# One weight cast moved behind the first norm, sixty unread products ahead of the first transposes, two means and one rounding moved, in a two-layer GNN kernel

## The chip, the cores and the metric

The kernel runs on one core of a Trainium2 chip. The metric is the device time of one execution in microseconds; the median over several executions is what versions are compared by. TensorE's clock has two levels, 1.2 and 2.4 GHz.

## The reference

The program has 1,250 nodes of 1,024 features, 20,000 edges sorted by destination, and two pre-norm layers with a residual each:

```python
h = relu(layernorm(x))
e = sigmoid(h @ wenc.T + benc)                 # 1250 x 500
agg = segment_sum((e @ conv)[src] * edge_weight, dst)
x = x + (agg + e @ lin.T) @ wdec.T + bdec
h = relu(layernorm(x))
y = h @ W.T + b                                # 1024 x 1024
x = x + gcn_normalized_sum_with_self_loops(y, src, dst)
```

Only the first line and the encoder product `h @ wenc.T` lie in the stretch that the change touches; the sparse adjacency is built beside them.

## The kernel before

All five engines run programs written out by hand; they meet only in semaphores (`wait_ge`, `then_inc`), and each engine executes strictly in the order of its own program. A `Signal` is a semaphore whose events must be raised in a listed order.

**Numbers in two parts.** Every fp32 operand of a product is split in a rounded high part (fp32r) and the remainder. For the activations these are `zhi` (ScalarE, `z_hi`) and `zlo` (VectorE, `z_lo`); for the four blocks of encoder weights `wehi` and `welo` (`wenc_lo`, VectorE). `wehi` 0 and 1 are cast by GpSimd, 2 and 3 by ScalarE (`wenc_hi`). A product of 1,024 long rows is three passes over eight slices: high by high, low by high, high by low.

**Blocks.** The nodes are ten blocks of 125 rows (`xn`, six buffers). For each block the first norm needs a mean and a variance: VectorE takes them for blocks 0, 1, 2 and 4 (`norm_stats`), ScalarE for the rest (`block_mean`, then `block_var`, into `wide`, about a microsecond each). `norm_step(n)` on VectorE turns the sums of two blocks into a scale and a shift by a chain of twelve tiny dependent instructions. `z_relu` (ScalarE) applies them in two halves; block 1 alone is done by VectorE (line 968, signal `relu_v`, without the ReLU, which `z_hi` makes up for). TensorE then transposes the block into PSUM (`turn_z`, eight transposes, line 1275), and `z_hi` and `z_lo` read it from there.

**Slots.** After the first two blocks the three big engines walk through a list of 30 slots: slots 0 to 19 are the encoder's (five groups of two blocks by four weight blocks), the last ten the conv product's. Slot s has on TensorE one encoder product (24 matmuls of 250 columns), the windows of adjacency batches listed in `adjs[s]`, and the transposes of a block (`turn_at`: blocks 2 and 3 in slot 3, block 4 in slot 6, block 5 in slot 7). The last pass of a product is held back until `zlo` is there. On ScalarE slot s has `enc_sigmoid(s)`, some means, variances and ReLUs, `z_hi` of the block transposed, and `adj_evac(u)`, which copies the finished window group u out of PSUM bank 3 + u % 3 (lines 642 and 643, tiles `C` and `A`). TensorE may start window group u only when group u - 3 is evacuated. On VectorE slot s has `hot_batch` (builds one-hot tiles `m_hot`, `s_hot` for the windows), `z_lo`, `norm_step`, `enc_lo(s)` (`hlo`, remainder of the sigmoid).

**Adjacency input.** Early TensorE products spread destination samples (`spread`), ScalarE counts them twice (`count_samples`, lines 593), VectorE makes row numbers (`find_windows`), GpSimd fetches edge rows by four indirect DMAs (`gather`: `sdw`, `ww`) and VectorE makes keys of them (`edge_keys`, `kf`).

The place where ScalarE starts, before the slots:

```python
        z_relu(0, 0)
        z_relu(0, 1)
        for k in range(2):
            for h in range(2):
                z_hi(k, h)
        block_mean(3)
        block_var(3)
        wenc_hi(2)
```

Of the kernel before, what the change touches and what calls it, by code (L numbers as in the profile page):

```python
# [20 lines left out]
FB = 4  # L21
# [18 lines left out]
SCRATCH = 4096  # L40
NXN = 6
NHOT = 3
BANKS = [(0, 0, 500), (1, 500, 1000), (2, 1000, 1250)]

SBUF0 = 4224
# [56 lines left out]
def build(nc, x, src, dst, ew, dst_s, sd_rows, w_rows, wenc, benc, conv, lin, wdec, W, b, out):  # L102
# [5 lines left out]
    def signal(name, events, by=1):  # L108
        return Signal(sem(name), events, by)
# [19 lines left out]
    identh = small("identh", [128, 128], F16, 2)  # L129
# [174 lines left out]
    def one(n):  # L304
        return [(i,) for i in range(n)]
# [36 lines left out]
    z_turned = signal("z_turned", BH)  # L342
    zhi_ok = signal("zhi_ok", BH)
    zlo_ok = signal("zlo_ok", BH)
    whi_p = signal("whi_p", one(2))
    whi_a = signal("whi_a", [(2,), (3,)])
    wlo_ok = signal("wlo_ok", one(FB))
    enc_done = signal("enc_done", GF)
    hhi_ok = signal("hhi_ok", GF)
# [167 lines left out]
    def gpsimd(p):  # L517
        p.memset(identf[:, :], 0.0).then_inc(*made_p.up("identf0"))
        p.wait_ge(*made_p.at("identf0"))
        p.affine_select(out=identf[:, :], in_=identf[:, :], compare_op=ALU.not_equal, fill=1.0, base=0,  # L520
                        pattern=[[-1, 128]], channel_multiplier=1).then_inc(*made_p.up("identf"))
        p.iota(thr[:, :], [[WD * HW, 2]], base=0, channel_multiplier=WD,
               allow_small_or_imprecise_dtypes=True).then_inc(*made_p.up("thr"))

        for g in range(NG - 1):
            p.memset(f32(hhi[g][:, 0, :]), 1.0).then_inc(*one_row.up(g))
        p.wait_ge(*d16_ok.at())
        p.iota(iota_s[:, :, :], [[1, 128], [0, GB]], base=0, channel_multiplier=0,
               allow_small_or_imprecise_dtypes=True).then_inc(*made_p.up("iota"))

        def gather(t):
            p.wait_ge(*row_ok.at(t))
            where = bass.IndirectOffsetOnAxis(ap=row_i[0:HW, t:t + 1], axis=0)
            p.indirect_dma_start(sdw[0:HW, t].rearrange("p a e -> p (a e)"), None, sd_rows, where
                                 ).then_inc(*d_gat[2 * t].up())
            p.indirect_dma_start(ww[0:HW, t, :], None, w_rows, where).then_inc(*d_gat[2 * t + 1].up())

        for f in range(2):
            p.wait_ge(*d_we[f].at())
            p.tensor_copy(wehi[f][:, :, :], we32[f][:, :, :]).then_inc(*whi_p.up(f))  # L540
        for t in range(2):
            gather(t)

        p.wait_ge(*flag_ok.at())
        general = p.value_load(flag[0:1, 0:1])
        with p.If(general > 0):
            p.wait_ge(*win_done.at(NWIN - 1))
            p.wait_ge(*conv_done.at(NB - 1))
            p.wait_ge(*edge_ok.at())
            p.iota(gi_d[0:PB, :], [[1, N]], base=0, channel_multiplier=0, allow_small_or_imprecise_dtypes=True  # L550
                   ).then_inc(*g_made.up(0))
            p.memset(gz[0:PB, :], 0.0).then_inc(*g_made.up(1))

        p.wait_ge(*win_done.at(NWIN - 1))
        p.wait_ge(*settled.at())
        p.memset(f32(ouhi[0][:, 0, :]), 1.0).then_inc(*one_row0.up())
        p.wait_ge(*A_put.at(NU - 1))
        p.wait_ge(*made_v.at("loops"))
        for k in range(NB):
            d_ap = C[0:PB, k, k * PB:(k + 1) * PB]  # L560
            p.tensor_tensor(d_ap, d_ap, loops[0:PB, 0:PB], ALU.add).then_inc(*diagC.up(k))

        def split_W(t):
            p.wait_ge(*Whi_ok.at(t))
            p.tensor_tensor(Wlo[t][:, :], W32[t][:, :], f32(Whi[t][:, :]), ALU.subtract).then_inc(*Wlo_ok.up(t))

        for k in range(NB - 1):
            for c in range(2):
                p.wait_ge(*t32_ok.at(k, c))
                cs = slice(512 * c, 512 * c + 512)  # L570
                p.tensor_tensor(glo[k][0:PB, cs], t32[(2 * k + c) % 4][0:PB, :], ghi[k][0:PB, cs], ALU.subtract
                                ).then_inc(*glo_p.up(k, c))
            if k == 1:
                split_W(0)
                split_W(1)
            if k == 3:
                split_W(2)
        for t in range(3, KB):
            split_W(t)
# [3 lines left out]
    def scalar(a):  # L583
# [33 lines left out]
        def z_hi(k, h):  # L617
            g, i = divmod(k, 2)
            a.wait_ge(*z_turned.at(k, h))
            if g >= 2:  # L620
                a.wait_ge(*enc_done.at(g - 2, FB - 1))
            a.activation(zhi[g % 2][:, 4 * h:4 * h + 4, i * PB:i * PB + PB],  # L622
                         ps[turn_bank(k, h)][:, 0:4 * PB].rearrange("p (k n) -> p k n", n=PB), ACT.Relu
                         ).then_inc(*zhi_ok.up(k, h))
# [29 lines left out]
        for k in range(2):  # L654
            for h in range(2):
                z_hi(k, h)
        block_mean(3)
        block_var(3)
        wenc_hi(2)
        for s, slot in enumerate(SLOTS):  # L660
            if s == 1:
                for k in range(2, 4):
                    for h in range(2):
                        z_relu(k, h)
                wenc_hi(3)
            if s == 2:
                for k in range(2, 4):
                    for h in range(2):
                        z_hi(k, h)
            if s in (2, 6, 7):  # L670
                k = {2: 5, 6: 5, 7: 8}[s]
                if s == 6:
                    z_relu(k, 0)
                    z_relu(k, 1)
                else:
                    block_mean(k)
                if s == 2:
                    block_var(k)
            done = [w // WD for i in adjs[s] for w in windows_of(i) if w % WD == WD - 1]
            for u in done[:(len(done) + 1) // 2]:  # L680
                adj_evac(u)
            if slot[0] == "enc":
                enc_sigmoid(s)
            for u in done[(len(done) + 1) // 2:]:
                adj_evac(u)
            if s == 5:
                a.wait_ge(*key_turn.at(0))
                a.activation(edge_k[:, :, :].rearrange("p k (t w) -> p (k t) w", t=2),
                             ps[3][:, :].bitcast(BF16)[:, 0:512].rearrange("p (k w) -> p k w", w=128)[:, :, 0:HW], ACT.Copy
                             ).then_inc(*edge_ok.up())  # L690
            if s in (5, 8, 9, 12, 13):
                k = {5: 4, 8: 6, 9: 7, 12: 8, 13: 9}[s]
                z_relu(k, 0)
                z_relu(k, 1)
            for k in range(4, NB):
                if turn_at[k] == s:
                    z_hi(k, 0)
                    z_hi(k, 1)
            if s in (3, 6, 9):
                block_mean({3: 6, 6: 7, 9: 9}[s])  # L700
            if s in (3, 6, 8, 10):
                block_var({3: 6, 6: 7, 8: 8, 10: 9}[s])
            if s in (17, 18):
                js = slice(2 * s - 34, 2 * s - 32)
                a.wait_ge(*d_cv.at())
                a.activation(cvhi[:, js, :], cv32[:, js, :], ACT.Copy).then_inc(*cvhi_ok.up(s - 17))
            if s == 19:
                a.wait_ge(*d_lin.at())
                a.activation(lnhi[:, :, :], ln32[:, :, :], ACT.Copy).then_inc(*lnhi_ok.up())
            if slot[0] == "conv":  # L710
                conv_evac_hi(slot[1])
# [101 lines left out]
    def vector(v):  # L813
# [64 lines left out]
                                       ).then_inc(*zlo_ok.up(k, h))  # L878

        def wenc_lo(f):  # L880
            v.wait_ge(*(whi_p if f < 2 else whi_a).at(f))
            v.tensor_tensor(welo[f][:, :, :], we32[f][:, :, :], f32(wehi[f][:, :, :]), ALU.subtract).then_inc(*wlo_ok.up(f))  # L882

        def enc_lo(s):
# [368 lines left out]
    def tensor(t):  # L1253
        def mm(o_ap, lhsT, rhs, start, stop):
            return t.matmul(o_ap, lhsT, rhs, start=start, stop=stop)  # L1255
# [34 lines left out]
        def enc(s, ws):  # L1290
            g, f = SLOTS[s][1:]
            i = g % 2
            o_ap = slot_bank(s)[0:PB, 0:GN]
            t.wait_ge(*(whi_p if f < 2 else whi_a).at(f))

            def one_pass(k, kind, start, stop):
                if kind == "lw" and g == 0 and k == 0:
# [21 lines left out]
        def first_hi(f):  # L1319

            o_ap = slot_bank(f)[0:PB, 0:GN]
            t.wait_ge(*(whi_p if f < 2 else whi_a).at(f))
            for k in range(KB):
                mm(o_ap, wehi[f][:, k, :], zhi[0][:, k, :], k == 0, False)
                mm(o_ap, wehi[f][:, k, :], zlo[0][:, k, :], False, False)
# [49 lines left out]
        for r in range(5):  # L1375
            ins = mm(ps[r][0:HW, 0:500], identh[0:5, r:r + 1].to_broadcast([5, HW]), d16[0:5, :], True, True)
        ins.then_inc(*spread.up())
        t.wait_ge(*made_p.at("identf"))
        turn_z(0)
        turn_z(1)  # L1380
# [314 lines left out]
```

## Time and profile before

| what | value |
|---|---|
| time, three runs | 501.79, 502.46, 503.77 us; median 502.46 us |
| the profiled execution | 501.87 us, of which span 500.1 us |
| busy TensorE matmul | 482.2 us, 96% of the span |
| busy VectorE, ScalarE, GpSimd | 252.3, 190.5, 56.1 us |
| the first matmul of the program, the first transpose | 3.32 us, 12.90 us |
| first encoder product; first adjacency window behind slot 8's encoder product | 16.41 us; 50.96 us |

In the profile a line number is that of the instruction's source; `PE` is TensorE's matmuls, `PEld` its weight loads, `DVE` VectorE, `ACT` ScalarE, `POOL` GpSimd. The figure in square brackets behind an instruction is how long its engine sat idle ahead of it and what ended that. The span starts with the first instruction, and the time outside it is 1.8 us here.

### The profile page before, as it was taken

The numbers are of one execution on the slowest core, as the hardware profiler recorded it, in microseconds if no ns is written. First come the engines' busy times: TensorE is split into PE (matmuls) and PEld (weight loads), VectorE is DVE, ScalarE is ACT, GpSimd is POOL, SyncE is SP. The second block draws the span as 40 slices with busy tenths as digits, with TensorE's granted clock in tenths as the row PEclk, the third lists the DMA queues.
The fourth block names the chain that finished last, engine by engine and source line by source line (L and its number), as shares of the span: only waits on it lengthen the run. The fifth ranks groups of instructions, "written<-read, shape, count | busy, mean of one in ns | idle before, by whom it ended". The sixth has DMA issues, their size and how long they took to land.

```text
span 500.1 us, 8576 instructions
## 1 busy us (share of the span) xinstructions
PE 482.2 (96%) x3907; PEld 428.2 (86%) x3407; DVE 252.3 (50%) x532; ACT 190.5 (38%) x398; POOL 56.1 (11%) x55
## 2 busy tenths in 40 slices
PE   1997999999999999999999999999999999999997
PEld 0997999988899999999878779987887897898775
DVE  6899687797439187122468995222122113112221
ACT  5898886664437205353324656510010010010000
POOL 4300000000040000000015733530000000000000
PEclk9999999999999999999999999999999999999999
DMA  8620004000000240000492001401101100200121
GB/s 309 223 85 2 1 3 146 21 1 1 2 3 1 43 178 1 0 2 1 170 346 75 1 3 46 167 1 41 42 1 41 42 1 22 62 1 20 42 52 50
DMA packets 9863, 28.17 MB, mean 56 GB/s; under 512 B 2444, under 2 KB 2505, under 8 KB 9691
## 3 DMA queue, kind: packets, MB, share of 16 engines
q1 hardware_dynamic: 9595, 27.15, 16.7%
q8 instruction: 33, 0.54, 0.5%
q0 software_dynamic: 224, 0.39, 0.3%
q14 instruction: 11, 0.09, 0.1%
HBM read 22.41 MB, written 5.12 MB: 55 GB/s over the span
## 4 chain that ended last, share of the span: by engine, by line
PE 89%; DVE 5%; ACT 3%; issue 1%; DMA 1%; SPq 0%; DVEq 0%
PE ps L1255 84%; PE ps L1259 2%; PE ps L1275 1%; ACT xn L615 1%; DMA xn<-in_x_dram 1%; DVE welo L882 1%; ACT wide L598 1%; PE ps L1491 1%; ACT wide L604 1%; PE ps L1490 1%; ACT zhi L622 1%; DVE zlo L876 0%; DVE rt L862 0%; DVE stats L828 0%; DVE stats L829 0%
## 5 line engine op out<-in xcount | busy, mean ns | idle before, releaser
L1255 PE MATMUL ps<-C,ghi 125*128 125x250 f16 x400 | 85.7, 270 | 0.0
L1255 PE MATMUL ps<-C,glo 125*128 125x250 f16 x400 | 85.6, 269 | 0.0
L1255 PE MATMUL ps<-Whi,Uhi 128*125 128x512 f32 x160 | 63.6, 398 | 0.0
L1255 PE MATMUL ps<-Wlo,Uhi 128*125 128x512 f32 x160 | 63.1, 394 | 0.0
L1255 PE MATMUL ps<-Whi,Ulo 128*125 128x512 f32 x160 | 63.0, 394 | 0.0
L806 ACT ACTIVATE Uhi<-ps 128x250 fp32r<-128x250 f32 x40 | 14.4, 382 | 124.3 <-PE ps L1255 124.3
L1248 DVE SCALAR_TENSOR_TENSOR x<-ps,dsc,x 125x512 f32<-125x512 f32 x20 | 15.0, 751 | 84.4 <-PE ps L1255 84.4
L1255 PE MATMUL ps<-Ahi,h2hi 125*125 125x250 f32 x200 | 56.4, 282 | 0.0
L1255 PE MATMUL ps<-Alo,h2hi 125*125 125x250 f32 x200 | 55.8, 279 | 0.0
L1255 PE MATMUL ps<-Ahi,h2lo 125*125 125x250 f32 x200 | 55.8, 279 | 0.0
L1233 DVE TENSOR_TENSOR Ulo<-ps,Uhi 128x250 fp32r<-128x250 f32 x40 | 16.1, 417 | 60.3 <-ACT Uhi L806 60.3
L1255 PEld LDWEIGHTS ps<-C,ghi 125*128 125x128 f16 x400 | 38.7, 97 | 5.1 <-issue 0.8
L1255 PEld LDWEIGHTS ps<-C,glo 125*128 125x128 f16 x400 | 38.9, 97 | 3.7
L1255 PE MATMUL ps<-zhi,wehi 128*125 128x250 f32 x160 | 40.6, 290 | 1.5 <-ACT zhi L622 1.5
L1255 PE MATMUL ps<-zlo,wehi 128*125 128x250 f32 x160 | 37.8, 279 | 0.0
L1255 PEld LDWEIGHTS ps<-Alo,h2hi 125*125 125x125 f32 x200 | 37.4, 187 | 0.0
L1255 PEld LDWEIGHTS ps<-Ahi,h2hi 125*125 125x125 f32 x200 | 37.3, 187 | 0.0
L1255 PEld LDWEIGHTS ps<-Ahi,h2lo 125*125 125x125 f32 x200 | 37.3, 186 | 0.0
L1255 PE MATMUL ps<-zhi,welo 128*125 128x250 f32 x160 | 36.4, 279 | 0.1
L1255 PEld LDWEIGHTS ps<-Whi,Ulo 128*125 128x125 f32 x160 | 29.7, 186 | 7.7
L1255 PEld LDWEIGHTS ps<-Whi,Uhi 128*125 128x125 f32 x160 | 29.6, 185 | 7.4
L1255 PEld LDWEIGHTS ps<-Wlo,Uhi 128*125 128x125 f32 x160 | 29.6, 185 | 7.3
(171 smaller groups left out, 1041.2 us busy)
## 6 DMA issues: line engine op xcount, KB each, us to landing
xn<-in_x_dram SPq DMA_DIRECT2D x10, 512.0 KB, 5.3
x<-in_x_dram SPq DMA_DIRECT2D x10, 512.0 KB, 8.7
out_dram<-x SPq DMA_DIRECT2D x20, 240.0 KB
W<-in_W_dram SPq DMA_DIRECT2D x8, 512.0 KB, 6.8
wd<-in_wdec_dram SPq DMA_DIRECT2D x1, 2048.0 KB, 8.1
we<-in_wenc_dram SPq DMA_DIRECT2D x4, 500.0 KB, 7.3
cv<-in_conv_dram SPq DMA_DIRECT2D x1, 1000.0 KB, 4.7
ln<-in_lin_dram SPq DMA_DIRECT2D x1, 1000.0 KB, 6.8
```

Of the source, the lines that this page charges most:

```text
L598: a.activation(wide[0:PB, 0], xn[k % NXN][0:PB, :], ACT.Copy, scale=1.0 / DIM, accum_out=mv[0:PB, k, 0:1]).then_inc(*sums_ok.up(k, "mean"))
L604: a.activation(wide[0:PB, 1], xn[k % NXN][0:PB, :], ACT.Square, scale=-1.0, bias=mv[0:PB, k, 0:1], accum_out=mv[0:PB, k, 1:2]).then_inc(*s ...
L615: a.activation(part, part, ACT.Relu, **kw).then_inc(*relu_a.up(k, h))
L622: a.activation(zhi[g % 2][:, 4 * h:4 * h + 4, i * PB:i * PB + PB], ps[turn_bank(k, h)][:, 0:4 * PB].rearrange("p (k n) -> p k n", n=PB), A ...
L806: a.activation(Uhi[u % 2][:, k, :], ps[bank8[item]][:, 0:GN], ACT.Copy).then_inc(*uhi_ok.up(u, k))
L882: v.tensor_tensor(welo[f][:, :, :], we32[f][:, :, :], f32(wehi[f][:, :, :]), ALU.subtract).then_inc(*wlo_ok.up(f))
L1233: v.tensor_tensor(Ulo[u % 2][:, k, :], ps[bank][:, 0:GN], f32(Uhi[u % 2][:, k, :]), ALU.subtract).then_inc(*ulo_ok.up(u, k))
L1248: v.scalar_tensor_tensor(r, ps[bank][0:PB, 0:512], col["dsc"][0:PB, k:k + 1], r, ALU.mult, ALU.add).then_inc(*out_ok.up(k, c))
L1255: return t.matmul(o_ap, lhsT, rhs, start=start, stop=stop)
L1259: return t.add_instruction(mybir.InstMatmult(name=nc.get_next_instruction_name(), engine=mybir.EngineType.PE, ins=[t.lower_ap(rhs), t.lowe ...
L1275: ins = t.transpose(ps[turn_bank(k, h)][:, j * PB:j * PB + PB], xn[k % NXN][0:PB, c:c + 128], identf[0:PB, 0:PB])
L1490: t.transpose(view[:, i * 128:i * 128 + PB], C[0:PB, k, j * PB:(j + 1) * PB], identh[0:PB, 0:PB])
```

## The change

Five edits, all of them in the first 50 us of the program:

1. GpSimd casts weight block 0 only after `relu_v`, that is after VectorE has finished `norm_step(0)` and block 1's norm; before, it cast as soon as the weights had arrived.
2. Weight block 1 is cast by ScalarE, between `z_hi(1, 1)` and `block_mean(3)`, no longer by GpSimd.
3. TensorE gets 60 products of 128 columns (identity by identity, fp16) into PSUM bank 7, which nothing reads, behind the `spread` products and ahead of the first transposes.
4. `block_mean(7)` moves from slot 6 to the end of slot 4, `block_mean(8)` from the head of slot 7 to its end.
5. `z_hi(5)` moves from the end of slot 7 to between the first evacuations and `enc_sigmoid(7)`.

```diff
+WARM = 60
@@ gpsimd
-        for f in range(2):
-            p.wait_ge(*d_we[f].at())
-            p.tensor_copy(wehi[f][:, :, :], we32[f][:, :, :]).then_inc(*whi_p.up(f))
+
+        p.wait_ge(*relu_v.at(1))
+        p.wait_ge(*d_we[0].at())
+        p.tensor_copy(wehi[0][:, :, :], we32[0][:, :, :]).then_inc(*whi_p.up(0))
         for t in range(2):
             gather(t)
@@ scalar
                 z_hi(k, h)
+        wenc_hi(1)
         block_mean(3)
         block_var(3)
         wenc_hi(2)
@@ scalar, in the loop over slots
-            if s in (2, 6, 7):
-                k = {2: 5, 6: 5, 7: 8}[s]
-                if s == 6:
-                    z_relu(k, 0)
-                    z_relu(k, 1)
-                else:
-                    block_mean(k)
-                if s == 2:
-                    block_var(k)
+            if s == 2:
+                block_mean(5)
+                block_var(5)
+            if s == 6:
+                z_relu(5, 0)
+                z_relu(5, 1)
             done = [w // WD for i in adjs[s] for w in windows_of(i) if w % WD == WD - 1]
             for u in done[:(len(done) + 1) // 2]:
                 adj_evac(u)
+            if s == 7:
+                z_hi(5, 0)
+                z_hi(5, 1)
             if slot[0] == "enc":
                 enc_sigmoid(s)
...
             for k in range(4, NB):
-                if turn_at[k] == s:
+                if turn_at[k] == s != 7:
                     z_hi(k, 0)
                     z_hi(k, 1)
-            if s in (3, 6, 9):
-                block_mean({3: 6, 6: 7, 9: 9}[s])
+            if s in (3, 4, 7, 9):
+                block_mean({3: 6, 4: 7, 7: 8, 9: 9}[s])
@@ tensor
         ins.then_inc(*spread.up())
+
+        for _ in range(WARM):
+            mm(ps[7][:, 0:128], identh[:, :], identh[:, :], True, True)
         t.wait_ge(*made_p.at("identf"))
         turn_z(0)
```

The signals `whi_p` and `whi_a` are relisted to match (block 0 by GpSimd, blocks 1 to 3 by ScalarE).

ScalarE at the start of the program, before: `xn` at line 615 is `z_relu`, `zhi` is `z_hi`, `wide` at 598 and 604 is a mean and a variance, `wehi` at 609 a weight cast, `h` and `hhi` the sigmoid.

```order
L593 ACTIVATE junk,cnt<-ps,thr_half 126x2500 x2
L615 ACTIVATE xn_130<-xn_130,nb,rstd 125x512 x2
L622 ACTIVATE zhi_128<-ps 128x4x125 x4
L598 ACTIVATE wide,mv<-xn_133 125x1024
L604 ACTIVATE wide,mv<-xn_133,mv 125x1024
L609 ACTIVATE wehi_124<-we_2_116 128x1000
```

The same place of the changed kernel, whose lines are two to three higher:

```order
L595 ACTIVATE junk,cnt<-ps,thr_half 126x2500 x2
L617 ACTIVATE xn_130<-xn_130,nb,rstd 125x512 x2
L624 ACTIVATE zhi_128<-ps 128x4x125 x4
L611 ACTIVATE wehi_123<-we_1_115 128x1000
L600 ACTIVATE wide,mv<-xn_133 125x1024
L606 ACTIVATE wide,mv<-xn_133,mv 125x1024
L611 ACTIVATE wehi_124<-we_2_116 128x1000
```

One cast of 1,000 columns (`wehi_123`) now stands ahead of block 3's mean and variance.

ScalarE from the end of slot 6 to the end of slot 7, before (`C` and `A` are an evacuation, `xn_131` block 7, `xn_132` block 8):

```order
L622 ACTIVATE zhi_128<-ps 128x4x125 x2
L598 ACTIVATE wide,mv<-xn_131 125x1024
L604 ACTIVATE wide,mv<-xn_131,mv 125x1024
L598 ACTIVATE wide,mv<-xn_132 125x1024
L642 ACTIVATE C<-ps 125x10x25
L643 ACTIVATE A_0_88<-ps 125x10x25
L642 ACTIVATE C<-ps 125x10x25
L643 ACTIVATE A_0_88<-ps 125x10x25
L631 ACTIVATE h_1_100<-ps,benc_t 125x250
L634 ACTIVATE hhi_110<-ps,benc_t 125x250
L642 ACTIVATE C<-ps 125x10x25
L643 ACTIVATE A_0_88<-ps 125x10x25
```

and of the changed kernel:

```order
L624 ACTIVATE zhi_128<-ps 128x4x125 x2
L606 ACTIVATE wide,mv<-xn_131,mv 125x1024
L644 ACTIVATE C<-ps 125x10x25
L645 ACTIVATE A_0_88<-ps 125x10x25
L644 ACTIVATE C<-ps 125x10x25
L645 ACTIVATE A_0_88<-ps 125x10x25
L624 ACTIVATE zhi_128<-ps 128x4x125 x2
L633 ACTIVATE h_1_100<-ps,benc_t 125x250
L636 ACTIVATE hhi_110<-ps,benc_t 125x250
L644 ACTIVATE C<-ps 125x10x25
L645 ACTIVATE A_0_88<-ps 125x10x25
L600 ACTIVATE wide,mv<-xn_132 125x1024
```

Two means are gone from ahead of the first evacuation, and `z_hi(5)` stands ahead of the sigmoid, where before it followed the last row of the piece.

## Rows read from the trace of the kernel before

**Rows 1.** The page: busy time, share of the span, instructions of TensorE.

```profile
PE 482.2 (96%) x3907; PEld 428.2 (86%) x3407; DVE 252.3 (50%) x532; ACT 190.5 (38%) x398; POOL 56.1 (11%) x55
```

**Rows 2.** Windows: stretch, length, busy PE, PEld, DVE, ACT, POOL, granted clock, DMA.

```profile
40.00:52.00 12.00, 9.48 (x131) 8.96 (x82) 11.49 (x31) 8.81 (x23) 0.00 (x0) 1.00 0.00 1
52.00:100.00 48.00, 47.91 (x677) 46.80 (x423) 37.06 (x79) 36.92 (x97) 0.00 (x0) 1.00 0.13 45
```

**Rows 3.** Timeline around the first norm step: start, duration (us), engine, instruction.

```profile
7.92 1.02 POOL L540 CAST wehi<-we 128x1000 fp32r<-128x1000 f32 x1 [3.15 <-DMA we<-in_wenc_dram]
8.06 0.89 DVE L840 TENSOR_SCALAR ve<-mv 125x2 f32<-125x2 f32 x1
...
9.12 1.02 POOL L540 CAST wehi<-we 128x1000 fp32r<-128x1000 f32 x1 [0.19 <-DMA we<-in_wenc_dram]
9.20 0.95 DVE L862 TENSOR_TENSOR rt<-ry 125x2 f32<-125x2 f32 x1
...
10.37 0.19 ACT L593 ACTIVATION_READ_ACCUMULATOR junk<-ps,thr_half 126x1 f32 x1
...
11.75 0.16 DVE L869 SCALAR_TENSOR_TENSOR nb<-mv,rstd 125x2 f32<-125x2 f32 x1
11.95 1.52 ACT L615 ACTIVATE xn<-xn,nb,rstd 125x512 f32<-125x512 f32 x2 [1.38 <-DVE nb L869]
11.95 0.81 DVE L968 TENSOR_SCALAR xn<-xn,rstd,nb 125x1024 f32<-125x1024 f32 x1
```

**Rows 4.** Timelines of TensorE: spread products, first and third transposes, fp16 transposes.

```profile
3.32 2.31 PE L1255 MATMUL ps<-d,identh 5*126 5x500 f16 x5 [3.32 <-DVE d L962]
...
12.90 1.07 PE L1275 MATMUL ps<-identf,xn 125*128 125x125 f32 x4 [7.28 <-ACT xn L615]
...
23.95 0.80 PE L1275 MATMUL ps<-identf,xn 125*128 125x125 f32 x6
...
217.36 0.22 PE L1490 MATMUL ps<-identh,C 125*125 125x125 f16 x1
217.42 0.22 PE L1491 MATMUL ps<-identh,C 125*125 125x125 f16 x1
```

**Rows 5.** Timeline from the first rounding to the second norm step.

```profile
14.01 0.59 ACT L622 ACTIVATE zhi<-ps 128x500 fp32r<-128x500 f32 x1 [0.54 <-PE ps L1275]
...
14.62 1.15 DVE L882 TENSOR_TENSOR welo<-we,wehi 128x1000 fp32r<-128x1000 f32 x1
...
15.68 2.43 DVE L876 SCALAR_TENSOR_TENSOR zlo<-ps,zhi 128x500 fp32r<-128x500 f32 x4
...
16.67 1.05 ACT L598 ACTIVATE wide<-xn 125x1024 bf16<-125x1024 f32 x1
...
18.99 1.02 ACT L609 ACTIVATE wehi<-we 128x1000 fp32r<-128x1000 f32 x1
...
19.19 0.21 DVE L840 TENSOR_SCALAR ve<-mv 125x1 f32<-125x1 f32 x2 [1.08 <-ACT wide L604]
```

**Rows 6.** Timeline, the third of four gathers, and the landing of such gathers.

```profile
16.94 1.00 POOL L534 DMA_INDIRECT sdw<-in_sd_rows_dram,row_i  x1 [0.31 <-issue]
...
DMA to landing us min/median/max: 4.9/5.2/5.5
```

**Rows 7.** Timeline of slots 5 to 8.

```profile
35.54 0.47 ACT L631 ACTIVATE h<-ps,benc_t 125x250 f32<-125x250 f32 x1 [0.68 <-PE ps L1255]
...
43.98 1.04 ACT L598 ACTIVATE wide<-xn 125x1024 bf16<-125x1024 f32 x1
...
45.70 0.22 PE L1255 MATMUL ps<-m_hot,s_hot 128*128 128x100 bf16 x1 [1.33 <-ACT A L643]
...
48.06 0.70 PE L1255 MATMUL ps<-zhi,wehi 128*125 128x250 f32 x4 [1.20 <-ACT zhi L622]
...
49.04 1.26 DVE L876 SCALAR_TENSOR_TENSOR zlo<-ps,zhi 128x500 fp32r<-128x500 f32 x2
...
50.01 1.10 PE L1255 MATMUL ps<-zlo,wehi 128*125 128x250 f32 x8
```

More of the change, by code:

```diff
@@ L344, in build @@
     zlo_ok = signal("zlo_ok", BH)
-    whi_p = signal("whi_p", one(2))
-    whi_a = signal("whi_a", [(2,), (3,)])
+    whi_p = signal("whi_p", [(0,)])
+    whi_a = signal("whi_a", [(f,) for f in range(1, FB)])
     wlo_ok = signal("wlo_ok", one(FB))
@@ L880, in wenc_lo @@
         def wenc_lo(f):
-            v.wait_ge(*(whi_p if f < 2 else whi_a).at(f))
+            v.wait_ge(*(whi_a if f else whi_p).at(f))
             v.tensor_tensor(welo[f][:, :, :], we32[f][:, :, :], f32(wehi[f][:, :, :]), ALU.subtract).then_inc(*wlo_ok.up(f))
@@ L1293, in enc @@
             o_ap = slot_bank(s)[0:PB, 0:GN]
-            t.wait_ge(*(whi_p if f < 2 else whi_a).at(f))
+            t.wait_ge(*(whi_a if f else whi_p).at(f))
             def one_pass(k, kind, start, stop):
@@ L1321, in first_hi @@
             o_ap = slot_bank(f)[0:PB, 0:GN]
-            t.wait_ge(*(whi_p if f < 2 else whi_a).at(f))
+            t.wait_ge(*(whi_a if f else whi_p).at(f))
             for k in range(KB):
```

## The prediction

> **What bounds the kernel now.** I read the page first. TensorE's matmuls are busy 482.2 us [rows 1] of a span of 500.1, so only 17.9 us are open at all, and the first transpose, at 12.90 us, comes after most of them. The table of windows says where the rest is: from 52 to 100 us TensorE is busy 47.91 of 48 us, from 40 to 52 only 9.48 of 12 while VectorE is busy 11.49 [rows 2]. So behind 52 us TensorE itself is the bound, and what the change can bring is how much earlier it passes 52 us. The timeline then names the gaps: 7.28 us ahead of the first transpose [rows 4], 1.33 us for an evacuation and 1.20 us for `zhi` of block 5 [rows 7]. Last, the chain of work that ended last and VectorE's timeline: from its start at 19.19 us, which waited 1.08 us for ScalarE's variance of block 3 [rows 5], VectorE works without a pause up to `z_lo(5)` at 49.04 us [rows 7]. Two chains must therefore move together: TensorE's, and VectorE's queue of 30 us, which feeds it with remainders.
>
> **The first norm (edit 1).** The two long rows of VectorE's tiny instructions, 0.89 and 0.95 us, end at 8.95 and 10.15 us, just as GpSimd's two casts do (8.94 and 10.14) [rows 3]. The nine steps behind them take from 10.15 to 11.91, 0.196 us each. I read this as VectorE standing still during each cast. The Trainium skill, SBUF — State Buffer, section "SBUF: two separate sides", says that VectorE and GpSimd share a pair of ports which one of them holds for a whole instruction; the trace agrees to 0.01 us in both rows. Without casts the twelve steps run from 8.06 at 0.2 us each, so `nb` starts at about 10.2 and is done at 10.4 instead of 11.91: 1.5 us. ScalarE, however, is done with its counting only at 10.56 [rows 3], so `z_relu(0,0)` starts at 10.6 instead of 11.95: **1.35 us** are left of it.
>
> The cast of block 0 now follows block 1's norm: that starts at 10.4, takes 0.81, so the cast runs from about 11.3 to 12.3. It will hold VectorE's `find_windows` up by about 1 us. VectorE comes to its next work 0.5 us earlier than before, not 1.5: `welo` from 14.1, the four `zlo` from 15.1 to 17.6 (before, 15.68 to 18.11) [rows 5]. `wehi(0)` is there at 12.3, wanted at about 14: hidden. Its remainder at 15.2 is wanted by TensorE at 14.6, so slot 0 has a new wait of about 0.7 us; this takes something from TensorE's lead, not from VectorE's.
>
> **The sixty products (edit 3).** Four transposes span 1.07 us at 12.90, so 0.21 us from one to the next; six span 0.80 us at 23.95, so 0.106 [rows 4]. The granted clock is printed as 1.00 in all windows, yet a factor of two lies between these rows: the first ran at 1.2 GHz, after 7.28 us without work, the later ones at 2.4. What the products must do is have the clock up before the first transpose. Their own length: five spread products of 500 columns take 2.31 us with the tail of the last, so 128 columns take at most 0.46 x 128 / 500 = 0.118; in a fast stretch two fp16 transposes with a load each start 0.058 apart [rows 4]. Sixty take 3.5 us if all are fast and at most 7.1 us if all are slow, from 5.6 to between 9.1 and 12.7. TensorE is wanted at 10.6 + 0.81 + 0.14 = 11.5, so the slow end would cost 1.2 us. I take the clock to rise part of the way through, since TensorE is then busy from 3.3 us on: end near 10.5, hidden. The Trainium skill, TensorE: Matmul & The Clock Gate, section "What's actually happening", says likewise that activity releases the throttle and idleness brings it back; the 7.28 us gap followed by half speed agrees.
>
> With the clock up the first four transposes are read 0.6 us after the first starts (3 x 0.106 + 0.27), where before it was 1.11 (12.90 to 14.01). So `z_hi(0,0)` is at 12.15. The second half's ReLU ends at 12.1, and its transposes at 12.85; then come `z_hi(0,1)` at 12.9, `z_hi(1,0)` at 13.4, `z_hi(1,1)` at 13.9, no longer waiting 0.84 us for each other as before. ScalarE is free at 14.35 instead of 16.67 [rows 5]: **2.3 us**, of which 1.35 are the norm's and about 0.95 the clock's.
>
> **The cast on ScalarE (edit 2).** It costs what its sister costs, 1.02 us, 0.93 from start to start [rows 5]. Its input has been there since 9.1 [rows 3]; its output, at 15.3, is wanted by slot 1 at about 18. So `block_mean(3)` starts at 15.3 instead of 16.67: 1.4 us earlier, and the variance releases `norm_step(1)` at 17.8 instead of 19.19. VectorE's own queue is done at 17.6, so ScalarE still sets the time, by 0.2 us. **VectorE's whole queue from 19.19 on moves by 1.4 us.** TensorE moves by about 1.2 in the same stretch: its last four products of slot 0 need the last `zlo` at 17.6, and end at 18.1, where slot 1 had started at 19.29.
>
> **Queues passed.** GpSimd's four gathers stand behind the cast, as they did. The row numbers come at about 12.4 and 12.7 instead of 13.0 and 13.3, so the third gather starts at 16.4 instead of 16.94; with 5.5 us to landing it is there at 21.9, and `edge_keys` asks at 23.7 - 1.4 = 22.3 [rows 6]. Hidden, by 0.4 us. No DMA is moved on SP; its reloads of `xn` wait for transposes and come earlier with them.
>
> **Means and rounding (edits 4, 5).** `block_mean(7)` goes where ScalarE had 0.68 us of idle time ahead of `enc_sigmoid(5)` [rows 7] and a little more ahead of `z_relu(4)`. The mean takes 1.2 us with its accumulator read, so `z_relu(4)` comes 1.0 us earlier than before instead of 1.2 to 1.4; its transposes in slot 6 have some 0.4 us to spare. Ahead of the first evacuation two means go, 2.2 to 2.4 us, which with the shift of 1.0 puts it at about 41.9 instead of 43.98 + 1.04 = 45.02 [rows 7]. The windows of its group are done by then, so the wait of 1.33 us [rows 7] disappears. Block 5's transposes then wait for `z_lo(4)`, which comes 1.4 us earlier like all of VectorE's queue, at 43.6, and end at 44.2; `z_hi(5)` follows them directly, and TensorE can begin slot 8 at about 44.4 instead of 48.06, so the 1.20 us are gone too. That is 3.6 us of lead, but slot 8 needs `z_lo(5)` for its last pass, and VectorE reaches that at 49.04 - 1.4 = 47.65: first half ready at 48.3, second at 48.9, then four products at 0.117 us [rows 7]. The pass that ended at 50.01 + 8 x 0.117 = 50.95 ends at 49.4. **The sum is 1.5 us**; of the 2.5 us of removed stalls nearly all turns up again as a wait for `zlo`, because VectorE's queue cannot move by more than its first start. Behind it TensorE is the bound and keeps what it has.
>
> From the profiled execution: 501.87 - 1.5 = 500.4, span 498.6. The profiled one lies 0.6 below the median of the three, so the median becomes 502.46 - 1.5 = **501.0 us**.
>
> **The rivals.**
> - *The clock doesn't hold.* TensorE is idle from about 10.5 to 11.5 again, after 7.28 us of idleness it was at 1.2 GHz. If the first transposes stay at 0.21 us, ScalarE's four `z_hi` end 0.95 us later, the cast eats the rest, and VectorE gains 1.4 - 0.95 = 0.4 us: 0.6 us in all, 501.9. Against it: 1 us is short beside 7.28. The Trainium skill's clock page says that the moment of the rise varies from run to run, which would make such executions a part of all.
> - *The gathers or the late cast hold VectorE up.* If the stall of `find_windows` is longer or the gathers land 1 us later, VectorE loses up to 0.7 us of its 1.4: gain 0.8, 501.7. For it: margins of 0.2 and 0.4 us only.
> - *Slower: the products are not hidden.* Should a product with its load cost as much as an fp32 transpose at 1.2 GHz, 0.21 us [rows 4], sixty end at 5.6 + 12.6 = 18.2, and the first transpose comes 5.3 us later than before (with the clock up, which gives 0.95 back): 506. It decides from 0.123 us per product on, where they end at 13.0. Against it: the two bounds from fp16 rows are 0.058 and 0.118.
> - *VectorE isn't the bound.* If it has slack in 19 to 49 us that the timeline hides, up to the full 3.6 us of slot 8's lead come through: 498.9. Against it are 11.49 busy us of 12 [rows 2].
> - *Nothing reaches the end:* later slots may be held by ScalarE or VectorE, which are busy 37 of 48 us each behind 52 us; then the lead is lost again, 502.4. TensorE's 47.91 of 48 speaks against it.
>
> **Chances.** Forecast (1.1 to 2.1 us gained) 0.60; clock 0.12; gathers or cast 0.09; slower 0.04; more than 2.5 us 0.10; nothing 0.05. A measurement of this kernel tells about 0.5%, 2.5 us, from no change. So faster 0.10, same 0.86, slower 0.04. The range, from part of the larger gain to the case of none, is 499.8 to 502.5.
>
> **What the profile after would show.** VectorE's steps at 8 to 10.4 us at 0.2 us each, `nb` at 10.2; `z_relu` at 10.6; sixty products from 5.6 to somewhere between 9.1 and 12.7, with a change of pace inside; the first four transposes spanning 0.6 us; GpSimd's cast at 11.3 and a long `find_windows` instruction beside it; `block_mean(3)` at 15.3; `norm_step(1)` at 17.8; `z_lo(5)` at 47.6 and a wait of TensorE of over 1.5 us for `zlo` in slot 8. The prediction is wrong if `z_lo(5)` moves by something other than 1.4 us, or if TensorE has new gaps behind 52 us.

## The result and the profile after

The changed kernel is slower. Its median is 504.55 us (22 executions) against 502.44 us (22 of the kernel before); the ratio is 1.0033, 95% interval 1.0017 to 1.0049. This ratio isn't the quotient of the two medians, which is 1.0042; the same holds for the ratios further down, so each gain in microseconds is given with what it was taken from. One of the 22 executions before took 1,549 us, which doesn't move their median. Forecast were 501.0 us and, most likely, no measurable change. The profiled execution is the fastest of the 22, 502.36 us with a span of 500.5, so its trace shows only part of the loss. The rest is in the list of spans and mean granted clocks, further down.

The page's first part, of the changed kernel, beside [rows 1]: sixty more matmuls and 5.5 us more of busy TensorE.

```profile
PE 487.7 (97%) x3967; PEld 432.4 (86%) x3467; DVE 248.7 (50%) x532; ACT 191.2 (38%) x399; POOL 54.3 (11%) x54
```

The timeline of the changed kernel around the first norm and the first transposes, beside [rows 3 to 5]:

```profile
5.56 5.38 PE L1258 MATMUL ps<-identh 128*128 128x128 f16 x60
...
7.86 0.17 DVE L843 TENSOR_SCALAR ve<-mv 125x2 f32<-125x2 f32 x1
...
10.02 0.16 DVE L872 SCALAR_TENSOR_TENSOR nb<-mv,rstd 125x2 f32<-125x2 f32 x1
...
10.46 1.51 ACT L617 ACTIVATE xn<-xn,nb,rstd 125x512 f32<-125x512 f32 x2
10.95 0.15 DVE L838 TENSOR_SCALAR cnt<-cnt 126x1 f32<-126x1 f32 x1
11.10 1.02 POOL L542 CAST wehi<-we 128x1000 fp32r<-128x1000 f32 x1 [6.34 <-DVE xn L971]
11.13 0.15 DVE L840 TENSOR_SCALAR row_i<-cnt 126x1 int32<-126x1 f32 x1
...
11.41 2.12 PE L1278 MATMUL ps<-identf,xn 125*128 125x125 f32 x16 [0.47 <-ACT xn L617]
...
12.06 2.20 ACT L624 ACTIVATE zhi<-ps 128x500 fp32r<-128x500 f32 x4
...
12.88 1.15 DVE L885 TENSOR_TENSOR welo<-we,wehi 128x1000 fp32r<-128x1000 f32 x1
...
15.06 1.07 ACT L600 ACTIVATE wide<-xn 125x1024 bf16<-125x1024 f32 x1
...
17.60 0.21 DVE L843 TENSOR_SCALAR ve<-mv 125x1 f32<-125x1 f32 x2 [1.22 <-issue]
```

The long rows of the first norm are gone, the sixty products end at 10.94, sixteen transposes span 2.12 us instead of 3.24, and the second norm step starts at 17.60 instead of 19.19. Slot 8, beside [rows 7], and the windows beside [rows 2] with the stretch around the second layer's start:

```profile
47.43 0.67 DVE L879 SCALAR_TENSOR_TENSOR zlo<-ps,zhi 128x500 fp32r<-128x500 f32 x1
...
48.15 1.31 PE L1258 MATMUL ps<-zlo,wehi 128*125 128x250 f32 x8 [1.72 <-DVE zlo L879]
```

```profile
40.00:52.00 12.00, 10.02 (x136) 9.09 (x82) 10.56 (x31) 8.04 (x21) 0.00 (x0) 1.00 0.00 1
52.00:100.00 48.00, 47.92 (x670) 46.41 (x416) 37.99 (x81) 36.92 (x98) 0.00 (x0) 1.00 0.13 44
296.00:302.00 6.00, 4.24 (x32) 3.35 (x31) 5.33 (x18) 2.75 (x4) 2.27 (x2) 1.00 0.02 7
```

TensorE reaches the windows behind slot 8 at 49.31 us (before, 50.96), and the second layer's first product at 297.61 (before, 299.08). Up to there 1.5 us are gained, as forecast. Then, in the trace of the kernel before:

```profile
299.08 0.28 PE L1255 MATMUL ps<-C,ghi 125*128 125x250 f16 x1
...
299.20 0.27 PE L1255 MATMUL ps<-C,glo 125*128 125x250 f16 x1
```

and in that of the changed kernel:

```profile
297.61 0.28 PE L1258 MATMUL ps<-C,ghi 125*128 125x250 f16 x1
299.65 0.27 PE L1258 MATMUL ps<-C,glo 125*128 125x250 f16 x1 [1.76 <-issue]
299.75 0.27 PE L1258 MATMUL ps<-C,ghi 125*128 125x250 f16 x1
```

One product runs, then TensorE stands for 1.76 us between two products whose operands had been there for long, and the reason given is `issue`: nothing that the profile knows. The place is the first after `with t.If(general > 0): u_and_w(True)`, that is after a jump over the skipped copy of the second layer's products (the copy that runs has about 2,500 matmuls and loads of TensorE). From 296 to 299.7 us the DMA view of the changed kernel has two packets of instructions, and that of queue q8 has 16 KB:

```profile
q8 instruction: 1, 0.02, 1.6%
q14 instruction: 1, 0.01, 0.7%
```

It starts at 297.48 us, 0.13 us ahead of the first product. The kernel before has such a packet too, at 299.00 us, 0.08 us ahead of its first product, and doesn't stall, so the packet alone explains nothing yet.

Last, the spans of the 22 executions fall in three groups: four of 500.5 to 501.0 us at a mean granted clock of 1.000, eight of 501.6 to 502.9 at 0.995 to 0.997, and ten of 503.5 to 504.3 at 0.992 or 0.993. Of 25 executions of the kernel before, taken beside the first experiment, sixteen had 499.6 to 500.7 at 0.999 or 1.000, seven 501.4 to 502.6 at 0.996 or 0.997, and two 502.8 and 503.2 near 0.992.

### The profile page after: what moved, and what is told of

The parts are those of the page before. It is cut to its first block, busy times and chain, and to the rows that moved or that the text cites. A ratio compares the mean times of both kernels' runs of the same rounds, so it can differ in the third digit from the quotient of the medians.

```text
span 500.5 us, 8697 instructions
## 1 busy us (share of the span) xinstructions
PE 487.7 (97%) x3967; PEld 432.4 (86%) x3467; DVE 248.7 (50%) x532; ACT 191.2 (38%) x399; POOL 54.3 (11%) x54
## 4 chain that ended last, share of the span: by engine, by line
PE 88%; DVE 3%; ACT 1%; issue 1%
PE ps L1258 84%; PE ps L1262 2%; PE ps L1278 1%; DVE m_hot L914 1%; PE ps L1497 1%; PE ps L1496 1%; DVE s_hot L911 0%; DVE zlo L879 0%; ACT xn L617 0%; DVE hlo L890 0%; ACT wide L606 0%; DVE m_hot L909 0%; DVE x L1251 0%; ACT C L644 0%; DVE edge_w L984 0%
```

## The experiments

All ratios are to the kernel before on the same chip. "Theory A" in the expectations is that the place of the code makes the stall, "theory B" that the clock does.

**The changed kernel again** (no edit).

> The changed kernel once more. In its first trace TensorE reached the second layer's first product at 297.6 us, 1.5 us earlier than before, and then stood still for 1.76 us with an idle reason of 'issue' one matmul behind a jump over a skipped branch. Theory A (code position: the 120 added TensorE instructions, 60 products with their loads, move the jump's target to the end of a block of code, and the next block is fetched too late): the same stall of 1.7 to 2.0 us at the same matmul in every trace; time 502 to 506. Theory B (the clock: the products or the gap behind them change when TensorE's clock falls): the stall is chance, and the granted clock of the slow executions is below 1.00 in one stretch that the trace will show. Both can be there.

504.47 us, ratio 1.0045 (1.0028 to 1.0062). The stall is at the same product, 2.3 us in its trace and so longer than expected. Of eight executions one was at clock 1.000 (span 500.9), five at 0.995 to 0.996 (502.2 to 502.9), two at 0.992 (503.5, 504.0). So the stall is no chance, and the clock adds to it.

**Without the products.**

```diff
-WARM = 60
+WARM = 0
```

> The changed kernel without the 60 unread products, all other edits kept. TensorE's code is then as long as before. Theory A: no stall behind the jump, and the first 50 us give 0.6 to 1.2 us, so 501.2 to 501.9 against 502.4. Theory B: the mean clock returns to that of the kernel before, 0.6 us gained as well; the two differ in whether the stall of 1.8 us is there (A: no; stall by chance or by early arrival: yes).

501.75 us, ratio 0.9982 (0.9967 to 0.9998), by the ratio 0.9 us faster. No stall at the jump: `ghi` product at 298.7, `glo` at 298.8. This speaks for the code's position, but not for it alone, since the products' own work is gone too.

**The changed kernel, the jump's target moved on.** Nothing that executes differs.

```diff
         with t.If(general > 0):
+            for _ in range(68):
+                mm(ps[7][:, 0:128], identh[:, :], identh[:, :], True, True)
             u_and_w(True)
```

> The changed kernel with 68 more products in TensorE's untaken branch of the second layer (the one for general edges), which never execute: with the 60 in front they are 128 products, 256 instructions of 64 bytes, 16 KB. Theory A: if blocks are 16 KB, the target of the jump is again where it was before within its block, the stall goes, and 1.4 to 1.6 us of gain appear: 500.9 to 501.1. Theory B: nothing changes, 504.5, as no executed instruction differs.

501.10 us, ratio 0.9972 (0.9960 to 0.9983). The stall is gone and the median is 3.4 us below that of the changed kernel beside it. This is what the prediction's sum had been for. Five of the twelve executions had a clock of 0.999 or 1.000 and spans of 498.4 to 498.8, seven 0.996 or 0.997 and 499.3 to 500.0. The profiled one is of the second kind; its windows over slot 8 (busy PE, PEld, DVE, ACT, POOL, then the granted clock):

```profile
47.00:48.00 1.00, 0.00 (x0) 0.00 (x0) 1.00 (x2) 0.06 (x1) 0.00 (x0) 1.00 0.00 0
48.00:49.00 1.00, 0.84 (x6) 0.78 (x7) 1.00 (x4) 0.00 (x0) 0.00 (x0) 1.00 0.00 0
49.00:50.00 1.00, 1.00 (x13) 0.79 (x7) 1.00 (x2) 0.00 (x0) 0.00 (x0) 0.56 0.00 0
50.00:51.00 1.00, 1.00 (x20) 0.76 (x7) 0.26 (x1) 0.61 (x3) 0.00 (x0) 0.50 0.00 0
51.00:52.00 1.00, 1.00 (x6) 1.00 (x6) 0.21 (x1) 1.00 (x4) 0.00 (x0) 0.50 0.00 0
```

TensorE idles for 1.73 us up to 48.16, waiting for `zlo`; about a microsecond after it has resumed the clock is at 1.2 GHz (0.50 of full), and it stays there to about 52.5.

**The kernel before, its jump's target moved on by 120 instructions.** The same edit with `range(60)` in the kernel before.

> The kernel before with 60 products in TensorE's untaken branch of the second layer, never executed: the jump's target is 120 instructions further on, as in the changed kernel. Theory A: a stall of 1.7 to 2.0 us behind the jump at 299 us, time 504.3, perhaps more if the clock suffers from the stall. Theory B: the time of before, 502.4, as no executed instruction differs.

506.12 us, ratio 1.0077 (1.0055 to 1.0100). Not one executed instruction differs from the kernel before, and it is 3.9 us slower, against an expected 1.9. The stall is 2.8 us here, where 1.7 to 2.0 were expected:

```profile
298.85 0.28 PE L1255 MATMUL ps<-C,ghi 125*128 125x250 f16 x1
301.93 0.27 PE L1255 MATMUL ps<-C,glo 125*128 125x250 f16 x1 [2.81 <-POOL glo L571]
```

The releaser named, GpSimd's `glo` of the first block, was made around 260 us in the trace of the kernel before: a case of an engine named that had long been done. Behind the stall, the windows show the second part of the loss:

```profile
302.00:303.00 1.00, 1.00 (x10) 0.92 (x10) 0.90 (x6) 0.00 (x0) 0.00 (x0) 0.95 0.00 0
303.00:304.00 1.00, 1.00 (x7) 0.71 (x6) 0.63 (x5) 0.70 (x2) 0.00 (x0) 0.50 0.08 16
304.00:305.00 1.00, 1.00 (x7) 0.71 (x6) 0.77 (x5) 1.00 (x2) 0.00 (x0) 0.50 0.00 0
305.00:306.00 1.00, 1.00 (x7) 0.71 (x6) 0.00 (x0) 1.00 (x3) 0.58 (x1) 0.50 0.00 0
306.00:307.00 1.00, 1.00 (x9) 0.88 (x8) 0.00 (x0) 1.00 (x2) 1.00 (x2) 0.84 0.00 0
```

The missing shares of the clock sum to 0.05 + 3 x 0.50 + 0.16 = 1.7 us. All six executions had a mean clock of 0.993 to 0.997.

**Position, three more places.** The kernel before with 64, then with 50 products in the untaken branch (the same edit with `range(64)` and `range(50)`):

> The kernel before with 64 products in the untaken branch, where 60 of them cost 3.9 us. Theory A: 502.2, no stall. A rule by which a longer skipped branch costs more: 506 or above.

> The kernel before with 50 products in the untaken branch: the target is 20 instructions ahead of that with 60, so ten more products of 0.107 us, 1.07 us of work, can run before the block ends. Theory A: the stall shrinks from 2.8 us to 1.7 to 1.8 us, and the time lies between 503 and 504.5, depending on whether the clock still falls behind it. If any position but the last few instructions is safe: 502.2.

And the changed kernel with 64 executed products instead of 60:

```diff
-WARM = 60
+WARM = 64
```

> The changed kernel with 64 unread products instead of 60, nothing else. Theory A (code position): in the changed kernel TensorE executed one product and one load behind the jump and then waited for the next block of code, so the target lay a few instructions ahead of a block's end. Eight instructions more put it at the start of the next block: no stall, 500.9 to 501.3. If not position but the number of products or the length of the program did it: 504.5 as with 60.

With 64 in the branch: 503.22 us beside 503.22, ratio 1.0005 (0.9990 to 1.0021), no stall. The expected 502.2 was missed in the absolute number only, since the kernel before itself was at 503.2 beside it. In this trace the clock falls in slot 8, behind the two waits of the kernel before, 1.32 and 1.19 us here (a timeline row, and rows of windows as above):

```profile
47.88 1.17 PE L1255 MATMUL ps<-zhi,wehi 128*125 128x250 f32 x4 [1.19 <-ACT zhi L622]
```

```profile
47.00:48.00 1.00, 0.12 (x1) 0.15 (x1) 1.00 (x4) 1.00 (x4) 0.00 (x0) 0.81 0.00 0
48.00:49.00 1.00, 1.00 (x5) 1.00 (x6) 1.00 (x3) 0.21 (x1) 0.00 (x0) 0.50 0.00 0
51.00:52.00 1.00, 1.00 (x10) 1.00 (x10) 0.69 (x1) 0.00 (x0) 0.00 (x0) 0.98 0.00 0
```

The four products span 1.17 us where they span 0.70 in the trace of the kernel before [rows 7]. With 50: 503.58 us, ratio 1.0019 (1.0005 to 1.0033), with a stall of 1.3 us, shorter than the expected 1.7 to 1.8; here too the clock falls in slot 8, at about 48.8, and not behind the stall. Its timeline is the sharpest evidence for the code's position. TensorE runs eleven products, from 301.17 to 302.25, and stands behind the eleventh:

```profile
301.17 0.28 PE L1255 MATMUL ps<-C,ghi 125*128 125x250 f16 x1
...
302.25 0.27 PE L1255 MATMUL ps<-C,ghi 125*128 125x250 f16 x1
303.79 0.27 PE L1255 MATMUL ps<-C,glo 125*128 125x250 f16 x1 [1.27 <-POOL glo L571]
```

With 60 it had run one. Ten products with their loads are 20 instructions, the very distance by which the target was moved. With 64 executed products the changed kernel takes 500.70 us, ratio 0.9963 (0.9948 to 0.9978): four products more, and the loss of 0.3 to 0.4% is a gain of 0.4%, a little more than expected.

**The gap in slot 8 filled**, first with 42 products in the untaken branch (so that 60 + 26 + 42 = 128), then with none:

```diff
+                if kind == "lz" and (g, f, k) == (2, 0, 0):
+                    t.wait_ge(*hhi_ok.at(1, 2))
+                    for _ in range(26):
+                        mm(ps[0][:, 0:128], identh[:, :], identh[:, :], True, True)
                 if kind == "lz" and f == 0 and k % 4 == 0:
```

> The changed kernel with its jump put right (42 products in the untaken branch) and 26 more unread products in slot 8, ahead of the first product that waits for the low part of block 5, where TensorE stood still for 1.7 us; 26 at 0.058 us fill 1.5 us of it. 60 + 26 + 42 are 128 products as in the kernel with 68 in the untaken branch, which took 501.1 us and in whose trace the clock fell to half from 49.4 to 52.5 us, behind that gap. Theory B2 (an idle stretch of this length brings the clock down in some executions): the mean clock is 0.999 to 1.000 in nearly all executions and the median 500.3 to 500.6. If the fall has nothing to do with the gap: the same 501.1, with 0.997 in half of them. If the products delay the pass: above 501.1.

> The changed kernel with 26 unread products in slot 8's wait and nothing in the untaken branch. The jump's target is then 52 instructions further on than in the changed kernel, and 172 further than before. Theory A (only the place of the target within its block of 256 instructions counts, and the block's end lay a few instructions behind the changed kernel's target): the target is well inside a block, no stall at the jump, 500.3 to 500.6 as with the padded variant, and nearly all executions at a mean clock of 0.999 or 1.000. If the length of the program or the added products themselves made the stall: 504 or above.

500.38 us, ratio 0.9957 (0.9940 to 0.9973), and 500.35 us, ratio 0.9953 (0.9936 to 0.9969). All fourteen executions had a mean clock of 0.998 to 1.000 and spans of 498.3 to 499.0; of the 24 of the two variants without fillers and without the stall (64 products, and 68 in the branch), twelve had. TensorE in the second of them:

```profile
46.31 1.62 PE L1258 MATMUL ps<-identh 128*128 128x128 f16 x26
48.19 0.73 PE L1258 MATMUL ps<-zlo,wehi 128*125 128x250 f32 x4 [0.26 <-DVE zlo L879]
```

The real product starts at 48.19, as with the gap open (48.15): the fillers cost nothing.

**The edits one by one**, each with the jump's target where it was before. The casts alone:

```diff
+        p.wait_ge(*relu_v.at(1))
+        p.wait_ge(*d_we[0].at())
+        p.tensor_copy(wehi[0][:, :, :], we32[0][:, :, :]).then_inc(*whi_p.up(0))
...
+        wenc_hi(1)
         block_mean(3)
```

> Edits 1 and 2 alone (GpSimd's cast of block 0 behind the first norm, block 1's cast on ScalarE); no unread products, means and rounding where they were. TensorE's code is as long as before. By the prediction's steps: the norm ends 1.5 us earlier, ScalarE gains 1.35 and pays 0.93 for the cast, so the second norm step starts 0.4 us earlier and the time falls by at most 0.4: 501.8 to 502.2. If the first norm is all that counts: 501.1 to 501.3.

502.37 us, ratio 1.0000 (0.9982 to 1.0018): no gain, where up to 0.4 us was expected. The means and the rounding alone:

```diff
+            if s == 7:
+                z_hi(5, 0)
+                z_hi(5, 1)
...
-            if s in (3, 6, 9):
-                block_mean({3: 6, 6: 7, 9: 9}[s])
+            if s in (3, 4, 7, 9):
+                block_mean({3: 6, 4: 7, 7: 8, 9: 9}[s])
```

> Edits 4 and 5 alone (two means and block 5's rounding moved). By the prediction, VectorE's queue sets when slot 8 gets its last operand, and that queue doesn't move: TensorE's waits of 1.33 and 1.20 us turn into one of over 2 us for the low part; gain 0.0 to 0.3 us, 501.9 to 502.3, and more executions in which the clock falls behind the longer wait. If ScalarE's waits were the bound: up to 2.5 us, 499.7 to 500.

502.53 us, ratio 0.9995 (0.9983 to 1.0007). That the clock would fall more often behind the longer wait didn't come true: 6 of these 12 executions have a mean clock of 0.996 or 0.997, and 14 of the 29 of the kernel before beside them one of at most 0.997. The products alone, with 68 more in the untaken branch:

```diff
         ins.then_inc(*spread.up())
+        for _ in range(60):
+            mm(ps[7][:, 0:128], identh[:, :], identh[:, :], True, True)
```

> The kernel before with only the 60 unread products, and 68 in the untaken branch so that the jump's target keeps its place in the block. By the prediction the clock is at its upper level for the first transposes and ScalarE is free 0.95 us earlier, which moves the second norm step by as much unless VectorE's own queue (four zlo, done at 18.1) holds it: it held it by 1.1 us less than ScalarE did, so 0.9 us: 501.2 to 501.5. If the products bring nothing: 502.2.

500.99 us, ratio 0.9975 (0.9962 to 0.9988): 1.3 us by the ratio, 1.5 by the medians, more than the 0.9 expected. All five edits with the stall away gave 501.10 (0.9972) and 500.70 (0.9963), so edit 3 alone brings most of it. With the casts alone the ReLU starts at 10.46, but the transposes are slow, ScalarE waits for each, and the cast eats what is left:

```profile
11.41 3.56 PE L1278 MATMUL ps<-identf,xn 125*128 125x125 f32 x16 [5.79 <-ACT xn L617]
...
12.51 0.59 ACT L624 ACTIVATE zhi<-ps 128x500 fp32r<-128x500 f32 x1 [0.54 <-PE ps L1278]
...
16.43 1.05 ACT L600 ACTIVATE wide<-xn 125x1024 bf16<-125x1024 f32 x1
...
18.95 0.21 DVE L843 TENSOR_SCALAR ve<-mv 125x1 f32<-125x1 f32 x2 [2.49 <-ACT wide L606]
```

With the products alone `norm_step(1)` starts at 17.95, with all edits at 17.60; in the five traces with neither casts nor products moved it starts between 19.0 and 19.4. With the means alone TensorE waits 1.7 us for `zlo` in slot 8, where before it had waited 1.33 and 1.20 elsewhere.

## Why the prediction was wrong

**The first 50 us were right, mostly to 0.2 us.** Forecast and found: `nb` 10.2 and 10.02; the first ReLU 10.6 and 10.46; products' end 10.5 and 10.94; ScalarE's first mean 15.3 and 15.06; `norm_step(1)` 17.8 and 17.60; `z_lo(5)` 47.65 and 47.43, so it moved by 1.6 us and not 1.4; the wait for `zlo` over 1.5 and 1.72; end of slot 8's pass 49.4 and 49.31; the second layer 1.5 us earlier. That VectorE's queue and not TensorE's gaps decides is shown by the means alone: two stalls of TensorE vanish and nothing is gained.

**The step that failed** is the last of the sum: "Behind it TensorE is the bound and keeps what it has." It was taken from busy shares, which say what TensorE did with the instructions it had. The change added 120 instructions to TensorE's program. I costed their time, found it hidden, and left out the place of all that stands behind them. This moved the target of the jump into the second layer to a few instructions ahead of the end of a block of code, and 1.76 to 2.3 us were lost there in its two traces (2.8 in the kernel before with the same shift), more than the 1.5 gained. The prediction itself had named new gaps of TensorE behind 52 us as a sign of being wrong. The experiments in which no executed instruction differs show it both ways: 60 products in the untaken branch cost the kernel before 3.9 us, 68 give the changed kernel 3.4 us. Against the kernel before, shifts of the target by 100 and by 120 instructions stall, behind eleven products and behind one; shifts by 0, 128, 172 and 256 don't. The Trainium skill, Runtime: NRT & Kernel Launch, section "Instruction fetch mechanics", has the rule: instructions are fetched in blocks of 16 KB, 256 of them, one ahead, and a taken branch to a target outside what is loaded has to fetch first. The traces agree: 16 KB packets, and a shift of 256 instructions that changes nothing.

The packets of q8 fit this. There are 35 of them in the changed kernel, 0.57 MB, and from 325 to 491 us one comes for every 235 to 278 matmuls and loads of TensorE, so the queue is TensorE's. Each of the fourteen traces has one 3.1 to 3.2 us ahead of the first product behind the jump, and a second between 0.2 us ahead of that product and 0.8 us behind it. In the four traces with a stall TensorE goes on 1.2 to 1.4 us after the second packet has ended (298.45 and 299.65 us in the changed kernel's). The traces don't say what a packet holds. That the first is the target's own block, and the second the block behind it, which is late if the target is near a block's end, is inferred. It accounts for the lengths of the stall: with 60 products in the branch the second packet starts 0.77 us behind the first product, in the changed kernel 0.13 us ahead of it (in its second trace 0.15, but it takes 1.47 us instead of 0.97), and with 50 it starts 0.25 us behind and ten more products cover part of it. Why its start varies stays open.

**The second step** is the rival on the clock, and with it the last line of the sum, which carries the 0.6 us between the profiled execution and the median over from the kernel before. I had weighed only whether the clock would be up for the first transposes. It was, in every trace with the products: the sixteen took 2.12 us, and 1.90 in the one where they began 0.2 us later. The distance became 2.2 us, since the clock falls later on, and each fall costs up to 1.7 us. Traces show two places. The one in slot 8 isn't new: of 96 executions of the kernel before, taken beside the experiments, 44 have a mean clock of at most 0.997, and two traces of it with an untaken branch made longer show the fall there, behind waits of 1.2 to 1.3 us. The change makes one wait of 1.7 us of them, and without the stall 12 of 24 executions still show a fall: no more often than before. The new place is the stall at the jump. Behind it the clock falls in the trace of the kernel before with 60 in the branch, and none of that kernel's six executions is above 0.997. Filling the wait in slot 8 took the falls away in fourteen of fourteen executions. The changed kernel has both places, and of its 30 executions 5 fit no fall, 13 fit one and 12 fit two. That the falls of its own slow executions lie at these two places is inferred from the other traces, since both its own have clock 1.00. Five of the 96 executions of the kernel before are near 0.992 without any stall at the jump, so there is at least one more place, which no trace shows.

In numbers: between the two profiled executions -1.47 us (up to the second layer's first product) and +1.92 (from there to the second product) make +0.45, where the times differ by 0.49. The medians lie 2.19 and 0.57 us above these executions, which adds 1.62; this part is a difference of measured times, put down to the clock, and no independent sum. Together they are the 2.1 us measured, and the 3.5 us by which the forecast was too low are the 1.92 and the 1.62.

**Smaller misses.** `find_windows` was to stand still for 1 us beside the late cast, and did not (0.15 us each, at 11.13, with the cast running from 11.10). So `welo` came at 12.88, not 14.1, VectorE's margin was 1.2 us instead of 0.2, and slot 0 got no wait for `welo` where 0.7 us was forecast; the one there is, 0.25 us at 21.1, is slot 1's. The clock was worth more than 0.95 us: 1.1 to 1.5 alone (17.95, against 19.01 to 19.41 in the five traces with neither) and 1.35 on top of the casts (18.95 to 17.60). The margin of the products was smaller than it looks: the change of pace from 0.107 to 0.056 us a product, which was to be inside them, came at about 9.5 us in the changed kernel's first trace, but only at about 11.2 us in that of the kernel with 26 products in slot 8 and none in the branch, where the first transpose started at 11.62 instead of 11.41. In the rival on the clock, 0.4 us for VectorE should have made 0.5 in all, by the way the main sum goes, not 0.6. The casts gave their 1.35 less 0.93 only with the clock up (17.95 to 17.60) and next to nothing alone, since with slow transposes ScalarE waits for TensorE.

## What to carry to other kernels

Count the instructions that an edit adds to an engine, not only their time: each jump behind them gets another place in its block of 256, and a target one or eleven products ahead of a block's end brought stalls of 1.3 to 2.8 us. When a harmless edit costs a few microseconds, pad an untaken branch and measure again, and look in the trace behind each jump for idle time put down to `issue` or to an engine that was done long before. TensorE's clock may fall behind a stall and add up to 1.7 us to it. It does so in some executions only, so a median can hold a loss that the profiled execution doesn't show: look at the list of spans and clocks too. Where a wait can't be removed, unread products in it kept the clock up at no cost, and the two kernels with 26 of them (500.35 and 500.38 us) are the fastest measured here.

## What the runs showed of the hardware

- VectorE's single-column instructions (126x1) ran at 0.15 us beside a GpSimd cast, while two-column ones (125x2: 0.89 in the trace of before) and those with two tensor inputs (0.95) stood until it ended [rows 3]. The Trainium skill, SBUF — State Buffer, section "SBUF: two separate sides", says that of VectorE's instructions those in a two-port mode and those with two inputs in SBUF contend. The rows with two tensor inputs agree; that the two-column rows with one input run in such a mode, and the single-column ones don't, is not tested by any run here.
- TensorE's clock fell to 1.2 GHz behind idle stretches of 1.2 to 2.8 us in some executions and not in others of the same kernel. By the windows it fell about 1 us after TensorE was busy again in two traces (68 in the branch of the changed kernel, 60 in that of the kernel before), about 0.5 us after in the trace with 50, and about 0.3 us before it was busy again in that with 64.
- TensorE stood still for 1.3 to 2.8 us behind a jump whose target lay one or eleven products ahead of the end of a block of 256 instructions, and not when it lay elsewhere; instructions that never execute moved the time by up to 3.9 us.
- The printed granted clock was 1.00 at 12.9 us in the kernel before, where transposes went at half the later rate. A row's pace tells the level there, the column doesn't.
